# A two-layer graph attention kernel: row masks in pieces of 512 columns behind the second exponential, and the values of two steps gathered together

## The chip, the cores and the metric

The kernel runs on one core of a Trainium2 chip. The metric is the device time of one launch in microseconds (us); lower is better. TensorE is called PE here, VectorE DVE, ScalarE ACT, GpSimd POOL; SP is the engine that issues the DMAs.

## What is computed

Two layers of the same form stand one behind the other, with N = 4096 nodes, 128 features, 8 heads of 16 and an adjacency matrix of 4096 x 4096 that masks the scores:

```python
qkv = layer_norm(x, g1, be1) @ w_qkv
qkv = qkv.reshape(n, 3, HEADS, HEAD_DIM)
q, k, v = (qkv[:, 0], qkv[:, 1], qkv[:, 2])
scores = jnp.einsum('nhd,mhd->hnm', q, k) * SCALE
mask = (adj != 0)[None, :, :]
scores = jnp.where(mask, scores, -jnp.inf)
attn = jax.nn.softmax(scores, axis=-1)
out = jnp.einsum('hnm,mhd->nhd', attn, v).reshape(n, DIM)
x = x + out @ w_proj + b_proj
h2 = layer_norm(x, g2, be2)
ff = jax.nn.gelu(h2 @ w1 + b1) @ w2 + b2
return x + ff
```

All of it is in float32.

## The kernel before

Each layer has three phases with a barrier between them: `project` makes queries, keys and values, `attend` is the attention, `feed_forward` the rest. Nearly all the time lies in `attend`, and the change touches nothing else.

The 4096 queries are cut into 8 blocks of 512 (`NB`), the keys into 32 slices of 128 (`MT`). `attend` does two kinds of work side by side.

The **max jobs** find the largest masked score of each query and head. A job is one matmul of 128 queries by 512 keys for one head (`a_job`, L386) into one of three PSUM banks (`A_BANKS`), and one custom instruction of DVE, with a read of its accumulator, that subtracts the row mask `mask_n` and takes the maximum (`take_max`, L736). A block has 256 jobs. After them DVE splits the maxima (`split_neg`), and four more jobs, called turns, transpose them (L393) and add them to the queries (`add_neg`). The row masks are made by ACT from loaded rows of the adjacency matrix, 1024 columns at a time (`mask_rows`, L624), in two slots; a piece serves 16 jobs.

The **steps** do the attention itself: 512 a layer (`STEPS`), 64 to a block, each with four heads (the first 32 steps of a block, its first half, have heads 0 to 3, the others heads 4 to 7) and one slice of 128 keys. In `b_step` PE first runs two max jobs, then computes the scores of heads 0 and 1 (L414) when the first exponential of the step before is done, adds the mask to them by a matmul with the identity (L420), then the scores of heads 2 and 3 when the second exponential of the step before is done, and a second part of the mask; then two more max jobs; and at the end `gather_v` of the step two before (`LAG`), which multiplies the probabilities by the values (L407), four matmuls side by side in four column strips, each of which the trace shows as two instructions:

```python
                if t >= LAG:
                    gather_v(L, t - LAG)
```

ACT takes two exponentials of 1024 columns a step (`exp_pair`, L608), the first of heads 0 and 1, the second of heads 2 and 3. POOL then multiplies the values of heads 2 and 3 by a mask of zeros and ones (`mask_pair`, L860), in place of the full mask matmul for these heads. In the first layer's first halves POOL also makes the masks from the adjacency matrix (L844, L850) and multiplies in every second step only, and PE adds the full mask in the others. `p_buf` has four slots. At the start of each half, in the step whose number divides by 32 with remainder 2, ACT copies the finished output of the half before (`keep_o`, L616) between the two exponentials; the first gather of a half waits for that copy.

The jobs run ahead of the steps by a block and some (`FIRST_JOBS`): 276 of them before the first step. So the last block of steps of each layer has no jobs beside it; there a step has another form, with the mask by matmuls of full height (L460).

Each engine works through its own queue in the order of the code. What binds them are semaphores, and where a mask piece stands on ACT follows from numbers: `chunk_step(i)` is the step in which PE reaches the first job of piece i, and `attend` of ACT makes the piece two steps ahead:

```python
                    exp_pair(L, t, 0)
                    if t > LAG and t % MT == LAG:
                        keep_o(L, t // MT - 1)
                    while chunk[0] < NCH and chunk_step(chunk[0]) - 2 < t + 1:
                        mask_rows(L, chunk[0])
                        chunk[0] += 1
                    exp_pair(L, t, 1)
```

SP issues all loads and stores from one sorted list, in which a load of adjacency rows (`load_n`) is due nine steps ahead of its jobs.

Of the kernel before, what the change touches and what calls it, by code (L numbers as in the profile page):

```python
# [27 lines left out]
NB = N // TILE  # L28
NS = TILE // P
MT = N // P  # L30
CHUNK = 1024
NC = N // CHUNK


# [6 lines left out]
P_SLOTS = 4  # L41
Q_SLOTS = 3
M_SLOTS = 6
LAG = 2
LEAD = 16

# [28 lines left out]


def chunk_jobs(nb, q, c):
    return JOB_AT["score", nb, q, 2 * c, 0], JOB_AT["score", nb, q, 2 * c + 1, HEADS - 1]


C_QK, C_V, C_PROJ, C_W1, C_W2 = 0, 1024, 1152, 1280, 1792
# [5 lines left out]
def gnn_kernel(nc, x, adj, adj_t, weights, signs, ident, ident_f, out):  # L87
    ctx = ExitStack()
    with ctx:
        def sb(name, shape, dt):  # L90
            return ctx.enter_context(nc.sbuf_tensor(name, shape, dt))
# [17 lines left out]
        q_t = sb("q_t", [P, Q_SLOTS, PAIRS, TILE], F32R)  # L109
        v_sb = sb("v_sb", [P, MT * HEADS * VW + 16], F32)  # L110
        v_rows = v_sb[:, 0:MT * HEADS * VW].rearrange("p (t h d) -> p t h d", t=MT, d=VW)
        adj_in = sb("adj_in", [P, 2, CHUNK], I32)
        mask01 = sb("mask01", [P, M_SLOTS, TILE], I32)
        mask_n = sb("mask_n", [P, 2, CHUNK], BF16)
        spill = sb("spill", [P, A_BANKS, TILE], BF16)
        pmax = sb("pmax", [P, 2, NS * HEADS, 8], F32)
        neg = sb("neg", [P, NS * HEADS], F32)
# [46 lines left out]
        q_stored = [sem("q_stored_0"), sem("q_stored_1")]  # L164

        q_loaded = [sem(f"q_loaded_{i}") for i in range(Q_SLOTS)]
        adj_loaded = [sem("adj_loaded_0"), sem("adj_loaded_1")]
        adjt_loaded = [sem(f"adjt_loaded_{i}") for i in range(M_SLOTS)]
        n_made, mask01_made, t_made, p_masked = sem("n_made"), sem("mask01_made"), sem("t_made"), sem("p_masked")
        m01_stored, mt_stored = [sem(f"m01_stored_{i}") for i in range(M_SLOTS)], sem("mt_stored")  # L170
# [46 lines left out]
        def _(sp):  # L217
# [5 lines left out]
            def load_n(L, i):  # L223
                sub, c = i // NC, i % NC
                gi = L * NCH + i
                if gi >= 2:
                    sp.wait_ge(n_made, gi - 1)
                sp.dma_start(adj_in[:, gi % 2, :], adj[sub * P:(sub + 1) * P, c * CHUNK:(c + 1) * CHUNK]).then_inc(adj_loaded[gi % 2], 16)

            def load_t(L, t):  # L230
                nb, s, slot = t // (2 * MT), t % MT, t % M_SLOTS
# [40 lines left out]
            for L in range(LAYERS):  # L272
# [17 lines left out]
                sp.wait_ge(q_stored[1], (L + 1) * NB // 2 * 16)  # L290
                phase_barrier(sp, 3 * L + 1)

                order = [(chunk_step(i) - 9, "n", i) for i in range(NCH)]
                order += [(t - M_SLOTS + 2.2, "t", t) for t in range(STEPS)]
                if L == 0:
                    order += [(t - 1, "s", t) for t in range(STEPS) if made(L, t)]
# [44 lines left out]
        def _(pe):  # L341
# [81 lines left out]
            def b_step(L, t):  # L423


                nb, quad, s = t // (2 * MT), t // MT % 2, t % MT
                jobs = range(jobs_before(t), jobs_before(t + 1))
                for j in jobs[:2]:
                    a_job(L, j)
                if L == 0:  # L430
                    pe.wait_ge(t_made, nb * MT + s + 1)
                else:
                    pe.wait_ge(mt_loaded[s % 4], (nb * MT + s) // 4 * 16 + 16)
                if t > 0:
                    pe.wait_ge(b_exped, L * 2 * STEPS + 2 * t - 1)
                if s == 0:
                    pe.wait_ge(a_done, L * NJ + JOB_AT["turn", nb, 2 * quad + 1] + 1)
                score_b(L, t, 0), score_b(L, t, 1)
                if len(jobs) >= 4:
                    add_mask(s, 0, 0), add_mask(s, 1, 1).then_inc(half_added, 1)  # L440
                    added[0] += 1
                    if t > 0:
                        pe.wait_ge(b_exped, L * 2 * STEPS + 2 * t)
                    score_b(L, t, 2), score_b(L, t, 3)
                    pe.wait_ge(half_added, added[0])
                    if pooled(L, t):
                        add_mask(s, 1, 0), add_mask(s, 0, 1).then_inc(b_scored, 2)
                        for j in jobs[2:]:
                            a_job(L, j)
                    else:  # L450
                        add_mask(s, 1, 0), add_mask(s, 0, 1).then_inc(b_scored, 1)
                        add_mask(s, 2, 0), add_mask(s, 3, 1).then_inc(half_added, 1)
                        added[0] += 1
                        for j in jobs[2:]:
                            a_job(L, j)
                        pe.wait_ge(half_added, added[0])
                        add_mask(s, 3, 0), add_mask(s, 2, 1).then_inc(b_scored, 1)
                else:
                    for j in range(2):
                        mm = pe.matmul(ps_b[:, j, :], idb[:], mask_t[:, s, :], start=False, stop=True)  # L460
                    mm.then_inc(b_scored, 1)
                    for j in jobs[2:]:
                        a_job(L, j)
                    if t > 0:
                        pe.wait_ge(b_exped, L * 2 * STEPS + 2 * t)
                    score_b(L, t, 2)
                    mm = score_b(L, t, 3)
                    if not pooled(L, t):
                        for j in range(2, 4):
                            mm = pe.matmul(ps_b[:, j, :], idb[:], mask_t[:, s, :], start=False, stop=True)  # L470
                    mm.then_inc(b_scored, 1)
                if t >= LAG:
                    gather_v(L, t - LAG)

            def attend(L):
# [85 lines left out]
        def _(act):  # L561
# [55 lines left out]

            def mask_rows(L, i):
                gi = L * NCH + i
                act.wait_ge(adj_loaded[gi % 2], (gi // 2 + 1) * 16)  # L620
                if i >= 2:
                    j = i - 2
                    act.wait_ge(a_done, L * NJ + chunk_jobs(j // NC // NS, j // NC % NS, j % NC)[1] + 1)
                nc.scalar.activation(mask_n[:, gi % 2, :], adj_in[:, gi % 2, :].bitcast(U32), ACT.Exp,  # L624
                                     bias=far[:], scale=MASKED).then_inc(n_made, 1)

            def attend(L):
                chunk = [0]
                while chunk_step(chunk[0]) < 1:
                    mask_rows(L, chunk[0])  # L630
                    chunk[0] += 1
                for t in range(STEPS):
                    exp_pair(L, t, 0)
                    if t > LAG and t % MT == LAG:
                        keep_o(L, t // MT - 1)
                    while chunk[0] < NCH and chunk_step(chunk[0]) - 2 < t + 1:
                        mask_rows(L, chunk[0])
                        chunk[0] += 1
                    exp_pair(L, t, 1)
                keep_o(L, 2 * NB - 1)  # L640

            def keep_attn(gi):
# [33 lines left out]
        def _(dve):  # L676
# [52 lines left out]

            def take_max(L, j):  # L730
                kind, nb, q, mb, h = JOBS[j]
                if h == 0 and mb % 2 == 0:
                    dve.wait_ge(n_made, L * NCH + (nb * NS + q) * NC + mb // 2 + 1)
                ca = L * NCH + (nb * NS + q) * NC + mb // 2
                dve.wait_ge(a_scored, L * NJ + j + 1)
                dve.tensor_tensor_reduce(spill[:, j % A_BANKS, :], ps_a[:, j % A_BANKS, :],  # L736
                                         mask_n[:, ca % 2, (mb % 2) * TILE:(mb % 2 + 1) * TILE],
                                         1.0, LOWEST, ALU.subtract, ALU.max,
                                         pmax[:, nb % 2, q * HEADS + h, mb:mb + 1]).then_inc(a_done, 1)

# [190 lines left out]
```

## Time and profile before

| | us |
|---|---|
| median of 3 runs | 4095.02 |
| lowest, highest | 4086.28, 4095.74 |
| the profiled execution, its own time | 4093.91 |
| its span, from the first to the last instruction | 4092.1 |
| busy: PE, DVE, POOL, ACT | 3621.1, 2945.0, 2481.3, 2445.5 |
| mean granted clock of PE, as a share of 2.4 GHz | 0.927 |

The page gives busy time, the chain of work that ended last, and the costliest groups of instructions. The timeline lists the instructions in order of time: start, length, engine, line, and in brackets how long the engine had been idle and what released it. Neighbours of one kind are merged, with their count. Starts of matmuls can be trusted more than their ends, which are modelled; so the text reads the distance from start to start.

### The profile page before, as it was taken

To read this page: it belongs to the slowest core of one execution; us is meant where nothing else is said; L and a number is where in the kernel's file an instruction comes from. 1 tells how busy PE (TensorE), PEld (TensorE's weight loads), DVE (VectorE), ACT (ScalarE), POOL (GpSimd) and SP (SyncE) were. 2 spreads that over 40 slices of the span, in tenths; PEclk is the share of its full clock that TensorE was granted. 3 is DMA by queue.
4 is the path that set the end of the run, shared out by engine and by line. 5 is a ranking of instruction groups with operands and counts; after the bars stand their busy time and mean duration, and the time that the engine had idled before them with its cause. 6 is when DMAs were issued, how large, how long until landed. Compare 5 with 4: busy or idle time off the path is not lost.

```text
span 4092.1 us, 66045 instructions
## 1 busy us (share of the span) xinstructions
PE 3621.1 (88%) x22382; PEld 1452.0 (35%) x22416; DVE 2945.0 (72%) x8933; ACT 2445.5 (60%) x2596; POOL 2481.3 (61%) x1476
## 2 busy tenths in 40 slices
PE   6999898989998989898679999889989998999976
PEld 3443333333333333323434433333333333333234
DVE  6998888888888888701368988888888888886013
ACT  5126666666666666675241166766676767676842
POOL 1017777777777777786010077777777777777940
PEclk9559999999999999998885599999999999999988
DMA  3236574747474747372232254545454545453421
GB/s 136 78 104 224 157 227 150 234 142 239 139 241 140 244 132 250 106 226 79 60 102 91 92 154 142 159 152 157 141 159 148 160 140 161 147 159 116 139 68 57
DMA packets 332878, 608.98 MB, mean 149 GB/s; under 512 B 35169, under 2 KB 125409, under 8 KB 328161
## 3 DMA queue, kind: packets, MB, share of 16 engines
q1 hardware_dynamic: 332112, 604.65, 46.8%
q8 instruction: 183, 3.00, 0.3%
q14 instruction: 151, 1.23, 0.1%
q10 hardware_dynamic: 432, 0.10, 0.0%
HBM read 474.59 MB, written 132.12 MB: 148 GB/s over the span
## 4 chain that ended last, share of the span: by engine, by line
POOL 34%; PE 29%; issue 18%; DVE 10%; ACT 6%; DMA 1%; POOLq 1%; DVEq 0%; SPq 0%; ACTq 0%
POOL arena L860 34%; DVE spill L736 9%; PE PS L407 8%; PE PS L386 6%; PE PS L414 6%; PE PS L420 5%; ACT mask_n L624 3%; PE PS L359 3%; ACT arena L608 2%; PE PS L393 1%; POOLq L838 1%; DVE neg_hi L745 0%; DVE arena L699 0%; PE PS L460 0%; DMA adj_in<-in_adj 0%
## 5 line engine op out<-in xcount | busy, mean ns | idle before, releaser
L736 DVE CUSTOM_DVE_ANT_0 spill<-PS,mask_n 128x512 bf16<-128x512 f32 x4096 | 2614.5, 688 | 480.1 <-PE PS L386 421.9
L860 POOL TENSOR_TENSOR arena<-arena,mask 128x1024 int32<-128x1024 int32 x896 | 2129.9, 2377 | 948.4 <-ACT arena L608 943.6
L608 ACT ACTIVATE arena<-PS 128x1024 f32<-128x1024 f32 x2048 | 2013.4, 1022 | 1013.5 <-PE PS L420 936.1
L386 PE MATMUL PS<-k_t,q_t 48*128 48x512 f32 x4096 | 1355.4, 564 | 60.9 <-DVE pmax L736 44.3
L407 PE MATMUL PS<-arena,v_sb 128*32 128x512 f32 x8192 | 1101.6, 610 | 42.1 <-POOL arena L860 33.0
L414 PE MATMUL PS<-q_t,k_t 50*128 50x512 f32 x4096 | 944.9, 469 | 189.1 <-ACT arena L608 188.7
L386 PEld LDWEIGHTS PS<-k_t,q_t 48*128 48x128 f32 x4096 | 586.0, 202 | 1023.9 <-DVE pmax L736 959.3
L420 PE MATMUL PS<-arena,idb 64*128 64x512 bf16 x4000 | 783.4, 393 | 0.0
L414 PEld LDWEIGHTS PS<-q_t,k_t 50*128 50x128 f32 x4096 | 396.3, 189 | 504.4 <-ACT arena L608 361.2
L624 ACT ACTIVATE mask_n<-adj_in,far 128x1024 bf16<-128x1024 uint32 x256 | 291.9, 1141 | 284.2 <-DVE pmax L736 276.9
L420 PEld LDWEIGHTS PS<-arena,idb 64*128 64x128 bf16 x4000 | 193.0, 96 | 436.1 <-issue 312.0
L736 DVE DVE_READ_ACCUMULATOR2_ANT pmax<- 128x1 f32 x4096 | 339.5, 83 | 0.0
L778 DVE RECIPROCAL arena<-PS 128x32 f32<-128x32 f32 x16 | 5.7, 357 | 443.2 <-PE PS L491 443.2
L844 POOL TENSOR_SCALAR mask<-mask 128x512 int32<-128x512 uint32 x256 | 156.9, 613 | 202.1 <-DMA mask<-in_adj_t 192.6
L407 PEld LDWEIGHTS PS<-arena,v_sb 128*32 128x32 f32 x8192 | 162.6, 108 | 322.3 <-issue 269.3
L833 POOL TENSOR_SCALAR arena<-arena 128x4 f32<-128x4 f32 x32 | 7.3, 228 | 403.1 <-DVE arena L690 403.1
L850 POOL TENSOR_SCALAR arena<-mask 128x512 bf16<-128x512 int32 x256 | 158.1, 618 | 37.6 <-POOL mask L844 34.1
L359 PE MATMUL PS<-arena,wts 128*128 128x512 f32 x256 | 115.5, 605 | 0.0
L570 ACT ACTIVATE arena<-PS,wts 128x512 f32<-128x512 f32 x32 | 24.9, 777 | 145.1 <-PE PS L512 99.5
L652 ACT ACTIVATE arena<-PS,wts 128x512 f32<-128x512 f32 x64 | 43.8, 687 | 106.2 <-PE PS L520 103.7
L491 PE MATMUL PS<-idf,arena 128*128 128x128 f32 x128 | 31.3, 427 | 68.2 <-DMA arena<-attn_dram 68.2
L460 PE MATMUL PS<-arena,idb 128*128 128x512 bf16 x238 | 74.6, 384 | 5.4 <-issue 5.4
(54 smaller groups left out, 1022.7 us busy)
## 6 DMA issues: line engine op xcount, KB each, us to landing
mask<-m_dram SPq DMA_DIRECT2D x768, 256.0 KB, 2.7
adj_in<-in_adj SPq DMA_DIRECT2D x256, 512.0 KB, 3.9
mask<-in_adj_t SPq DMA_DIRECT2D x256, 256.0 KB, 3.8
m_dram<-mask SPq DMA_DIRECT2D x256, 256.0 KB, 3.5
mt_dram<-arena SPq DMA_DIRECT2D x256, 128.0 KB, 3.2
arena<-mt_dram SPq DMA_DIRECT2D x256, 128.0 KB, 2.7
q_dram<-arena SPq DMA_DIRECT2D x16, 1024.0 KB, 4.5
q_t<-q_dram SPq DMA_DIRECT2D x16, 1024.0 KB, 6.8
```

The source lines that it names most:

```text
L359: pe.matmul(PS[:, 2 + i % 4, :], wts[:, C_QK + i * P:C_QK + (i + 1) * P], xn_t[:, gx % 2, :], start=True, stop=True).then_inc(qk_ready, 1)
L386: pe.matmul(bank, q_t[r0:r0 + KROWS, (L * NB + nb) % Q_SLOTS, pair, q * P:(q + 1) * P], k_t[r0:r0 + KROWS, pair, mb * TILE:(mb + 1) * TILE ...
L407: mm = pe.matmul(ps_o[32 * j:32 * j + 32, :], v_sb[:, (s * HEADS + h) * VW:(s * HEADS + h) * VW + 32], p_buf[:, t % P_SLOTS, j, :], start= ...
L414: return pe.matmul(ps_b[:, j, :], k_t[r0:r0 + BROWS, pair, s * P:(s + 1) * P], q_t[r0:r0 + BROWS, (L * NB + nb) % Q_SLOTS, pair, :], start ...
L420: return pe.matmul(ps_b[:, j, :], idb[r0:r0 + 64, :], mask_t[r0:r0 + 64, s, :], start=False, stop=part != j % 2)
L460: mm = pe.matmul(ps_b[:, j, :], idb[:], mask_t[:, s, :], start=False, stop=True)
L608: nc.scalar.activation(p_buf[:, t % P_SLOTS, 2 * half:2 * half + 2, :], ps_b[:, 2 * half:2 * half + 2, :], ACT.Exp, scale=SCALE).then_inc( ...
L624: nc.scalar.activation(mask_n[:, gi % 2, :], adj_in[:, gi % 2, :].bitcast(U32), ACT.Exp, bias=far[:], scale=MASKED).then_inc(n_made, 1)
L736: dve.tensor_tensor_reduce(spill[:, j % A_BANKS, :], ps_a[:, j % A_BANKS, :], mask_n[:, ca % 2, (mb % 2) * TILE:(mb % 2 + 1) * TILE], 1.0, ...
L844: pool.tensor_scalar(m, m.bitcast(U32), 1.0, 0.0, ALU.min, ALU.max).then_inc(mask01_made, 1)
L850: pool.tensor_scalar(mask_t[:, s, :], m, -MASKED, MASKED, ALU.mult, ALU.add).then_inc(t_made, 1)
L860: pool.tensor_tensor(p, p, m, ALU.mult).then_inc(p_masked, 1)
```

## The change

It has two parts. Both are in `attend`.

**Row masks.** `CHUNK` falls from 1024 to 512, so that a piece serves 8 jobs and there are 256 pieces a layer in place of 128; the slots go from two to four (`N_SLOTS`), of half the size each. On ACT a piece now stands behind the second exponential of a step and three steps ahead of its jobs. SP loads it ten steps ahead.

**Values.** PE gathers in odd steps only, and then for two steps: those three and two before.

```diff
-CHUNK = 1024
+CHUNK = 512
+N_SLOTS = 4
...
-    return JOB_AT["score", nb, q, 2 * c, 0], JOB_AT["score", nb, q, 2 * c + 1, HEADS - 1]
+    return JOB_AT["score", nb, q, c, 0], JOB_AT["score", nb, q, c, HEADS - 1]
...
-        adj_in = sb("adj_in", [P, 2, CHUNK], I32)
+        adj_in = sb("adj_in", [P, N_SLOTS, CHUNK], I32)
-        mask_n = sb("mask_n", [P, 2, CHUNK], BF16)
+        mask_n = sb("mask_n", [P, N_SLOTS, CHUNK], BF16)
...
-                if gi >= 2:
-                    sp.wait_ge(n_made, gi - 1)
-                sp.dma_start(adj_in[:, gi % 2, :], adj[sub * P:(sub + 1) * P, c * CHUNK:(c + 1) * CHUNK]).then_inc(adj_loaded[gi % 2], 16)
+                if gi >= N_SLOTS:
+                    sp.wait_ge(n_made, gi - N_SLOTS + 1)
+                sp.dma_start(adj_in[:, gi % N_SLOTS, :],
+                             adj[sub * P:(sub + 1) * P, c * CHUNK:(c + 1) * CHUNK]).then_inc(adj_loaded[gi % N_SLOTS], 16)
...
-                order = [(chunk_step(i) - 9, "n", i) for i in range(NCH)]
+                order = [(chunk_step(i) - 10, "n", i) for i in range(NCH)]
...
-                if t >= LAG:
+                if t % 2 == 1 and t > LAG:
+                    gather_v(L, t - LAG - 1)
                     gather_v(L, t - LAG)
...
-                act.wait_ge(adj_loaded[gi % 2], (gi // 2 + 1) * 16)
-                if i >= 2:
-                    j = i - 2
+                slot = gi % N_SLOTS
+                act.wait_ge(adj_loaded[slot], (gi // N_SLOTS + 1) * 16)
+                if i >= N_SLOTS:
+                    j = i - N_SLOTS
...
-                while chunk_step(chunk[0]) < 1:
+                while chunk_step(chunk[0]) < 3:
...
-                    while chunk[0] < NCH and chunk_step(chunk[0]) - 2 < t + 1:
+                    exp_pair(L, t, 1)
+                    while chunk[0] < NCH and chunk_step(chunk[0]) - 3 < t + 1:
                         mask_rows(L, chunk[0])
                         chunk[0] += 1
-                    exp_pair(L, t, 1)
...
-                if h == 0 and mb % 2 == 0:
-                    dve.wait_ge(n_made, L * NCH + (nb * NS + q) * NC + mb // 2 + 1)
-                ca = L * NCH + (nb * NS + q) * NC + mb // 2
+                ca = L * NCH + (nb * NS + q) * NC + mb
+                if h == 0:
+                    dve.wait_ge(n_made, ca + 1)
```

The order of PE's queue in the second layer, before: one step, from its first max jobs (L386) over scores (L414) and masks (L420) to the gather (L407).

```order
L386 MATMUL PS<-k_t,q_t 128x512 x2
L414 MATMUL PS<-q_t,k_t 128x512 x2
L420 MATMUL PS<-arena,idb 128x512 x2
L414 MATMUL PS<-q_t,k_t 128x512 x2
L420 MATMUL PS<-arena,idb 128x512 x2
L386 MATMUL PS<-k_t,q_t 128x512 x2
L407 MATMUL PS<-arena,v_sb 32x512 x4
```

The same place in the changed kernel, where the lines are two further down: two steps, an even one without and an odd one with a gather of eight matmuls.

```order
L388 MATMUL PS<-k_t,q_t 128x512 x2
L416 MATMUL PS<-q_t,k_t 128x512 x2
L422 MATMUL PS<-arena,idb 128x512 x2
L416 MATMUL PS<-q_t,k_t 128x512 x2
L422 MATMUL PS<-arena,idb 128x512 x2
L388 MATMUL PS<-k_t,q_t 128x512 x4
L416 MATMUL PS<-q_t,k_t 128x512 x2
L422 MATMUL PS<-arena,idb 128x512 x2
L416 MATMUL PS<-q_t,k_t 128x512 x2
L422 MATMUL PS<-arena,idb 128x512 x2
L388 MATMUL PS<-k_t,q_t 128x512 x2
L409 MATMUL PS<-arena,v_sb 32x512 x8
```

The gather of the even step has gone into the odd one, and the last two jobs of the even step now stand directly ahead of the first two of the odd step.

The order of ACT's queue in the second layer about a copy of the output (L616), before: exponentials are L608, mask pieces L624.

```order
L624 ACTIVATE mask_n<-adj_in,far 128x1024
L608 ACTIVATE arena<-PS 128x1024 x2
L616 COPY o_sb<-PS 128x512
L608 ACTIVATE arena<-PS 128x1024 x6
L624 ACTIVATE mask_n<-adj_in,far 128x1024
```

The same place in the changed kernel (exponentials L611, copy L619, mask pieces L628):

```order
L628 ACTIVATE mask_n<-adj_in,far 128x512
L611 ACTIVATE arena<-PS 128x1024 x3
L619 COPY o_sb<-PS 128x512
L611 ACTIVATE arena<-PS 128x1024
L628 ACTIVATE mask_n<-adj_in,far 128x512
L611 ACTIVATE arena<-PS 128x1024 x4
```

A piece now follows four exponentials, or two steps, and the copy, which belongs to an even step, is followed by that step's second exponential and then by a piece: the pieces stand at the end of even steps.

## Rows read from the trace of the kernel before

**Rows 1.** The page, part 1: busy us, share of the span, instructions

```profile
PE 3621.1 (88%) x22382; PEld 1452.0 (35%) x22416; DVE 2945.0 (72%) x8933; ACT 2445.5 (60%) x2596; POOL 2481.3 (61%) x1476
```

**Rows 2.** The page, part 4: shares of the chain that ended last

```profile
POOL 34%; PE 29%; issue 18%; DVE 10%; ACT 6%; DMA 1%; POOLq 1%; DVEq 0%; SPq 0%; ACTq 0%
```

**Rows 3.** Timeline, second layer: start, us, engine, line, op, out<-in, count, idle before

```profile
3011.01 1.94 ACT L608 ACTIVATE arena<-PS 128x1024 f32<-128x1024 f32 x2 [0.82 <-PE PS L420]
...
3011.14 1.07 PE L407 MATMUL PS<-arena,v_sb 128*32 128x512 f32 x8
...
3012.14 0.50 PE L386 MATMUL PS<-k_t,q_t 48*128 48x512 f32 x2
...
3012.47 0.40 PE L414 MATMUL PS<-q_t,k_t 50*128 50x512 f32 x2
...
3013.00 0.50 PE L414 MATMUL PS<-q_t,k_t 50*128 50x512 f32 x2
...
3013.35 0.39 PE L420 MATMUL PS<-arena,idb 64*128 64x512 bf16 x2
...
3013.78 1.03 ACT L608 ACTIVATE arena<-PS 128x1024 f32<-128x1024 f32 x1 [0.83 <-PE PS L420]
...
3014.70 1.14 ACT L624 ACTIVATE mask_n<-adj_in,far 128x1024 bf16<-128x1024 uint32 x1
...
3017.58 1.94 ACT L608 ACTIVATE arena<-PS 128x1024 f32<-128x1024 f32 x2 [0.82 <-PE PS L420]
```

**Rows 4.** Groups by line: out<-in shapes xcount, busy, mean ns, idle before

```profile
L624 ACT ACTIVATE mask_n<-adj_in,far 128x1024 bf16<-128x1024 uint32 x256 | 291.9, 1141 | 284.2 <-DVE pmax L736 276.9
...
L583 ACT ACTIVATE arena<-PS,sgn 128x512 fp32r<-128x512 f32 x64 | 44.0, 687 | 12.4 <-PE PS L359 12.4
```

**Rows 5.** Chain in order of time, start of the first layer's attention

```profile
103.68 6.44 DMA adj_in<-in_adj
```

**Rows 6.** Timeline: second wave of a gather, and the job behind it

```profile
2999.49 0.61 PE L407 MATMUL PS<-arena,v_sb 128*32 128x512 f32 x4
...
3000.04 0.50 PE L386 MATMUL PS<-k_t,q_t 48*128 48x512 f32 x2
```

**Rows 7.** Timeline, first layer: scores, and the next first exponential

```profile
805.79 0.40 PE L414 MATMUL PS<-q_t,k_t 50*128 50x512 f32 x2
...
806.94 1.94 ACT L608 ACTIVATE arena<-PS 128x1024 f32<-128x1024 f32 x2 [0.88 <-PE PS L420]
```

**Rows 8.** Stretches: busy us (count) of PE, PEld, DVE, ACT, POOL; PEclk, DMA

```profile
2997.05:3057.00 59.95, 55.17 (x400) 20.60 (x400) 51.34 (x161) 43.42 (x46) 47.15 (x21) 1.00 0.50 157
```

**Rows 9.** Timeline, first layer, first half: gathers four steps apart

```profile
999.82 1.07 PE L407 MATMUL PS<-arena,v_sb 128*32 128x512 f32 x8
...
1012.55 0.64 PE L407 MATMUL PS<-arena,v_sb 128*32 128x512 f32 x4
```

**Rows 10.** Timeline, last block without max jobs: one step

```profile
1869.62 0.50 PE L414 MATMUL PS<-q_t,k_t 50*128 50x512 f32 x2
...
1870.05 0.61 PE L460 MATMUL PS<-arena,idb 128*128 128x512 bf16 x2
...
1870.59 0.50 PE L414 MATMUL PS<-q_t,k_t 50*128 50x512 f32 x2
...
1870.69 1.94 ACT L608 ACTIVATE arena<-PS 128x1024 f32<-128x1024 f32 x2 [0.46 <-PE PS L460]
...
1871.02 1.06 PE L407 MATMUL PS<-arena,v_sb 128*32 128x512 f32 x8
```

**Rows 11.** Timeline, change of half: copy, second exponential, waiting gather

```profile
814.42 0.58 ACT L616 COPY o_sb<-PS 128x512 f32<-128x512 f32 x1
...
814.89 1.04 ACT L608 ACTIVATE arena<-PS 128x1024 f32<-128x1024 f32 x1
...
815.15 1.06 PE L407 MATMUL PS<-arena,v_sb 128*32 128x512 f32 x8 [1.46 <-POOL arena L860]
```

**Rows 12.** Stretches, columns as in rows 8: after the stall of a block change

```profile
3147.00:3152.00 5.00, 5.00 (x32) 3.04 (x32) 2.35 (x5) 1.08 (x2) 0.18 (x1) 0.66 0.27 79
```

More of the change, by code:

```diff
@@ L166, in gnn_kernel @@
         q_loaded = [sem(f"q_loaded_{i}") for i in range(Q_SLOTS)]
-        adj_loaded = [sem("adj_loaded_0"), sem("adj_loaded_1")]
+        adj_loaded = [sem(f"adj_loaded_{i}") for i in range(N_SLOTS)]
         adjt_loaded = [sem(f"adjt_loaded_{i}") for i in range(M_SLOTS)]
@@ L619, in mask_rows @@
                 gi = L * NCH + i
-                act.wait_ge(adj_loaded[gi % 2], (gi // 2 + 1) * 16)
-                if i >= 2:
-                    j = i - 2
+                slot = gi % N_SLOTS
+                act.wait_ge(adj_loaded[slot], (gi // N_SLOTS + 1) * 16)
+                if i >= N_SLOTS:
+                    j = i - N_SLOTS
                     act.wait_ge(a_done, L * NJ + chunk_jobs(j // NC // NS, j // NC % NS, j % NC)[1] + 1)
-                nc.scalar.activation(mask_n[:, gi % 2, :], adj_in[:, gi % 2, :].bitcast(U32), ACT.Exp,
+                nc.scalar.activation(mask_n[:, slot, :], adj_in[:, slot, :].bitcast(U32), ACT.Exp,
                                      bias=far[:], scale=MASKED).then_inc(n_made, 1)
@@ L731, in take_max @@
                 kind, nb, q, mb, h = JOBS[j]
-                if h == 0 and mb % 2 == 0:
-                    dve.wait_ge(n_made, L * NCH + (nb * NS + q) * NC + mb // 2 + 1)
-                ca = L * NCH + (nb * NS + q) * NC + mb // 2
+                ca = L * NCH + (nb * NS + q) * NC + mb
+                if h == 0:
+                    dve.wait_ge(n_made, ca + 1)
                 dve.wait_ge(a_scored, L * NJ + j + 1)
                 dve.tensor_tensor_reduce(spill[:, j % A_BANKS, :], ps_a[:, j % A_BANKS, :],
-                                         mask_n[:, ca % 2, (mb % 2) * TILE:(mb % 2 + 1) * TILE],
+                                         mask_n[:, ca % N_SLOTS, :],
                                          1.0, LOWEST, ALU.subtract, ALU.max,
```

## Prediction

> **What bounds the kernel now.** I read the busy shares first, then the chain, then the timeline of single steps. No engine is full: PE 88%, DVE 72%, POOL 61%, ACT 60% [rows 1]. The chain puts 34% on POOL's multiplication and 29% on PE [rows 2], which looks like a POOL bound, but the timeline says otherwise. Rows 3 show an ordinary step of the second layer, and every step of that kind reads the same. ACT starts the two exponentials of a step at 3011.01; one row shows both, 1.94 us together. At 3013.00 PE starts the scores of heads 2 and 3 of the next step, which need the second exponential; at 3013.35 it adds the mask; at 3013.78 ACT starts again, having idled 0.8 us. So the loop is ACT, PE, ACT, and takes 2.77 us. Beside it PE runs its own row of work in those same 2.77 us: gather at 3011.14, two max jobs at 3012.14, scores at 3012.47, some 0.25 us for the mask, and then a wait of only about 0.2 us for ACT. Two limits thus stand almost level: **ACT's loop at 2.77 us, and PE's queue at about 2.7 us**. Every fourth step is longer: 1024 columns of row masks (1.14 us) stand on ACT between the two exponentials, and the step takes 3.80 us (3013.78 to 3017.58) [rows 3]. Four steps take 3 x 2.77 + 3.80 = 12.1 us, or 6.05 a pair.
>
> **Part one, the masks move and are halved.** The second exponential no longer stands behind a mask, which takes away 1.03 us from every fourth step. What is late next there is the ordinary loop of 2.77. A piece of 512 columns now stands behind the second exponential in every second step. The order puts it into even steps nearly throughout (the copy of o_sb, in a step that divides to 2, comes two instructions ahead of one). There ACT idles 0.8 us. How long does a piece take? From below, half of 1.14, or 0.57; from above 1.14; the nearest row is an activation of 512 columns with a bias operand, 0.69 us [rows 4], which I take. It overlaps its neighbour by some 0.1 us, as the second exponential starts 0.92 after the first, so it ends within the idle time; at 1.14 it would run 0.1 us or so over. The skill gives the same: the Trainium skill (ScalarE: Activation LUTs, What ACT_TABLE_LOAD costs) states about 280 ns + 0.833 ns an element with a bias operand, which is 1133 ns for 1024 columns, where this trace has 1141, and an estimate of 707 ns for 512. The 256 additional DMA issues lie on SP's queue, whose issues are not on the chain but for the first; 2 KB rows take the place of 4 KB ones. Masks wait for work of DVE four pieces back, about eight steps, and are loaded seven steps before use: no new wait. The very first load of a layer is on the chain for 6.44 us [rows 5] with four loads of 512 KB issued in a row; with half the bytes I estimate 2 us less, so **-4 us** for both layers (between 0 and -6).
>
> **Part two, two gathers in a row.** This removes one gather (about 1.0 us of PE) from every even step and puts it into the odd one. In an even step the first limit, ACT's loop, stays: 2.77 us, and PE idles a good microsecond. In an odd step PE's queue decides. What does the second gather add? A gather is two waves of four matmuls; the second wave starts at 2999.49 and the next job at 3000.04 [rows 6], so 0.55 of the 1.00 us from 3011.14 to 3012.14 [rows 3] is second wave and way out, 0.45 the first. Two more waves at 0.45 add 0.91, and the way out is paid once: 1.90 us for both. At the worst it adds a whole 1.00. Then, from the start of the first exponential of an odd step: 0.13 to the gather, 1.90, then 0.33 for two jobs up to the scores [rows 3], then from those scores to the next exponential where PE does not wait, 805.79 to 806.94, or 1.15 [rows 7]. That makes **3.51 us**. With the even step, 3.51 + 2.77 = **6.28 us a pair against 6.05**: the loss of overlap costs more than the mask stall gave.
>
> What the page on tiling says speaks for the change: the Trainium skill (TensorEngine Tiling (Array Packing), Key Properties) states that a change of tiling mode drains TensorE, and a gather is in another mode than all around it, so paired gathers halve such changes. The rows show a drain of about 0.1 us at the way out, which the 1.90 has already credited; if the drain were nothing, the pair would be at 6.37.
>
> DVE: 80 jobs of two instructions took 51.3 us in a stretch of 60 [rows 8], 0.64 each, so 8 want 5.1 of the 6.28 us. While PE gathers twice, DVE has three banks at most and idles about a microsecond. In the even step four jobs then stand in a row on PE, the last of which waits until DVE has done two of them; it comes about when the first exponential ends, for which PE would wait anyway. I take 0, and 0.1 us a pair at the worst. POOL gets more time: 4.8 us of work a pair, and values of an even step are needed one step later.
>
> **The sum.** Seven of eight column blocks of each layer carry max jobs.
> - Second layer and second halves of the first: 224 + 112 pairs x 0.23 = **+77**.
> - First halves of the first layer, where POOL also makes masks: from gather to gather four steps take 12.73 us [rows 9], 6.36 a pair; the new odd and even steps have the same limits as above, 6.28: 112 x -0.08 = **-9**.
> - Blocks without jobs (the last, 64 steps a layer): a step is 2.40 now. PE's row of work there, with s for scores and m for masks: 1.00 for the gather as in rows 3, 0.43 s, 0.54 m, 0.43 to the gather [rows 10]. With two gathers: 0.43 + 1.90 + 0.43 + 0.54 = 3.30 from the second scores to the next. In the even step the first scores wait for an exponential that starts 0.1 after and takes 1.02, then 0.43 and 0.54: 2.15. Together 5.45 against 4.80: 48 pairs x 0.65 = **+31**; the 16 pairs of the first layer's first half, slower already, I count at nothing (up to +10).
> - Change of half: the output is copied on ACT and the next gather waits 1.46 us for it [rows 11], on PE's path. Now the copy runs in an even step and the gather comes a step later, so only the 0.47 stays by which the second exponential starts later. 14 changes x -1.0, and two in the last blocks: **-16**.
> - Change of block: PE waits for DVE's maxima, and POOL works 0.18 us of 5 [rows 12]. Copy and jobs shift somewhat within that stall: 0, with 14 x 1.46, or 20 us, either way.
> - First loads **-4**.
> Sum 77 - 9 + 31 - 16 - 4 = **+79**. The profiled execution took 4093.9 us, about 1 us less than the median of the runs, so I forecast **4174 us**, 1.9% slower.
>
> **Rivals.**
> (1) The second gather is covered, so that both steps stay at ACT's 2.77, and only the mask stall goes. For it: the chain names POOL and ACT far more than gathers. It would give 168 groups of four steps x 1.02 and 56 x 1.65 less, -264 us with the -20 above: about 3810. Against it: PE waits 0.2 us in a step, not 0.9. Between this and the forecast lies every case in which the second gather adds less; the point from which the sign turns is 79 / 464 pairs = 0.17 below 0.91, that is 0.74 us for two waves that take 0.91 now. Chance 0.09 for faster, 0.06 for within 0.3%, about what a measurement can tell from no change.
> (2) PE's clock falls. After the stall at a change of block the granted clock is 0.66 in 5 us [rows 12], between the levels 2.4 and 1.2 GHz, and matmuls take up to twice as long. PE would now idle a good microsecond in 6.3, against about one in 12 now. If one pair in ten ran at the lower level, its 3.4 us of PE work in the odd step doubles: 46 x 3.4 = +156, so 4330. Against it: the present stalls of about 1 us behind the masks left the clock at 1.00 in that stretch [rows 8]. The Trainium skill (TensorE: Matmul & The Clock Gate, A second HAM failure mode: psum-queue depth-cycling) tells of a kernel whose clock oscillated through frequent short idles; no row here shows it. Chance 0.08.
> (3) The mask piece does not fit into the idle time of the even step (its first wait is for a load or for DVE, or it takes 1.14): 0.1 us in 448 pairs, +45, 4220. Chance 0.07.
> (4) The forecast as worked out, chance 0.70.
>
> **Chances and range.** Faster 0.09, within 0.3% 0.06, slower 0.85. The second gather at 1.00 gives +42, DVE's banks +45, blocks -20 to +20, tail -15 to +10, first loads a little: 4135 to 4235 about the forecast. To leave out two in ten I take 4125 to 4240.
>
> **What would show it.** First exponentials of a pair 3.5 and 2.8 us apart, gathers as 16 matmuls within 1.9 us with no wait ahead, then scores, and ACT idling some 1.6 us in odd steps for PE's mask matmul; no mask piece between two exponentials, each some 0.7 us; PE's busy share down, POOL idling 0.7 us a step; steps of the last block 3.3 and 2.15; no gather waiting for a copy. It is wrong if the odd step takes under 3.3 us, if the even one takes over 2.9 (DVE or masks), or if the granted clock falls below 0.9 in mid block.

## The result and the profile after

The changed kernel takes 4167.35 us (median of 4 runs, 4159.95 to 4176.57) against 4094.52 us before: the ratio is 1.018, with a 95% interval of 1.016 to 1.021. It is slower by 73 us. The forecast was 4174 us, in a range of 4125 to 4240.

The page of the changed kernel, part 1 (busy us, share of the span) and part 4 (shares of the chain):

```profile
PE 3772.3 (91%) x22416; PEld 1603.9 (39%) x22416; DVE 2906.9 (70%) x8933; ACT 2495.9 (60%) x2852; POOL 2480.3 (60%) x1476
...
POOL 33%; PE 30%; issue 19%; DVE 15%; DMA 1%; ACT 1%; POOLq 1%; DVEq 0%; SPq 0%; ACTq 0%
```

They answer to [rows 1, 2], and neither tells what happened. The shares of the chain differ by five points at most, and PE's busy share has even risen, from 88 to 91%. The timeline of the second layer tells it; here are an even and an odd step of the changed kernel, and the start of the next even one. Columns: start, length, engine, line, form, count, idle before.

```profile
3041.75 1.94 ACT L611 ACTIVATE arena<-PS 128x1024 f32<-128x1024 f32 x2 [1.53 <-PE PS L422]
...
3043.57 0.72 ACT L628 ACTIVATE mask_n<-adj_in,far 128x512 bf16<-128x512 uint32 x1
3043.74 0.19 PEld L416 LDWEIGHTS PS<-q_t,k_t 50*128 50x128 f32 x2 [0.30 <-ACT arena L611]
...
3044.51 1.94 ACT L611 ACTIVATE arena<-PS 128x1024 f32<-128x1024 f32 x2 [0.22 <-PE PS L422]
3044.64 1.92 PE L409 MATMUL PS<-arena,v_sb 128*32 128x512 f32 x16
...
3046.49 0.51 PE L388 MATMUL PS<-k_t,q_t 48*128 48x512 f32 x2
...
3046.84 0.40 PE L416 MATMUL PS<-q_t,k_t 50*128 50x512 f32 x2
...
3047.59 1.91 PE L388 MATMUL PS<-k_t,q_t 48*128 48x512 f32 x4
...
3047.98 1.94 ACT L611 ACTIVATE arena<-PS 128x1024 f32<-128x1024 f32 x2 [1.53 <-PE PS L422]
```

The even step runs from 3041.75 to 3044.51, 2.76 us. Its mask piece stands behind both exponentials, takes 0.72 us, and ACT still idles 0.22 us. PE waits 0.30 us for the second exponential there (3043.74; PEld is PE's weight load), so ACT's loop sets this step. The odd step runs to 3047.98, 3.47 us: PE gathers from 3044.64 to 3046.49, then makes two jobs, scores and masks, and ACT idles 1.53 us. The pair is 6.23 us against 6.05 before [rows 3]. The row at 3047.59 also shows why PE's busy share rose. Four max jobs in a row are listed with 1.91 us, where two take 0.50: the weight loads of the third and fourth wait for DVE, 0.43 us each, and the merged row counts that as busy.

The place that answers to [rows 11], the change of half:

```profile
2889.31 1.02 ACT L611 ACTIVATE arena<-PS 128x1024 f32<-128x1024 f32 x1 [1.52 <-PE PS L422]
2890.23 0.58 ACT L619 COPY o_sb<-PS 128x512 f32<-128x512 f32 x1
2890.70 1.04 ACT L611 ACTIVATE arena<-PS 128x1024 f32<-128x1024 f32 x1
...
2892.57 1.94 ACT L611 ACTIVATE arena<-PS 128x1024 f32<-128x1024 f32 x2 [0.23 <-PE PS L422]
2892.70 1.92 PE L409 MATMUL PS<-arena,v_sb 128*32 128x512 f32 x16
```

This even step takes 3.26 us, 0.50 more than an ordinary one, and the gather at 2892.70 waits for nothing. Not every change of half went so well. In seven of the fourteen beside max jobs, and at the start of two blocks, TensorE's granted clock fell to the level of 1.2 GHz for a few us, and the odd step behind the copy took 4.6 to 5.2 us, in place of 3.47 at a change of half. One such place, the gather and the stretch about it (span, busy us of PE, PEld, DVE, ACT, POOL, then the granted clock), and for comparison a stretch in mid block:

```profile
1022.82 3.48 PE L409 MATMUL PS<-arena,v_sb 128*32 128x512 f32 x16
...
1022.70:1026.20 3.50, 3.50 (x18) 0.59 (x16) 1.31 (x4) 1.94 (x2) 3.11 (x2) 0.55 0.60 173
3050.00:3110.00 60.00, 57.38 (x390) 22.84 (x390) 47.85 (x153) 43.35 (x49) 45.94 (x20) 1.00 0.49 141
```

The kernel before had such falls too, at four changes of half and the start of one block, all in the second layer. At a change of block PE waits for DVE in both kernels, 2.81 us before and 2.80 now at the places shown. Two gathers now stand behind this wait, and they run at the lower level. The gather behind the wait before, then in the changed kernel, with the clock of its stretch:

```profile
3146.21 1.06 PE L407 MATMUL PS<-arena,v_sb 128*32 128x512 f32 x8
...
3179.60 3.64 PE L409 MATMUL PS<-arena,v_sb 128*32 128x512 f32 x16
...
3178.00:3182.00 4.00, 3.12 (x13) 0.88 (x17) 2.53 (x8) 0.43 (x1) 2.25 (x1) 0.50 0.59 161
```

The last block, which answers to [rows 10]:

```profile
3990.91 1.94 ACT L611 ACTIVATE arena<-PS 128x1024 f32<-128x1024 f32 x2 [0.30 <-PE PS L462]
3994.17 1.94 ACT L611 ACTIVATE arena<-PS 128x1024 f32<-128x1024 f32 x2 [1.32 <-PE PS L462]
3996.40 1.94 ACT L611 ACTIVATE arena<-PS 128x1024 f32<-128x1024 f32 x2 [0.30 <-PE PS L462]
```

3.26 and 2.23 us, 5.49 a pair against 4.80.

### The profile page after: what moved, and what is told of

It is laid out like the page before. It is cut to its first block, busy times and chain, and to the rows that moved or that the text cites. A ratio compares the mean times of both kernels' runs of the same rounds, so it can differ in the third digit from the quotient of the medians.

```text
span 4165.8 us, 67099 instructions
## 1 busy us (share of the span) xinstructions
PE 3772.3 (91%) x22416; PEld 1603.9 (39%) x22416; DVE 2906.9 (70%) x8933; ACT 2495.9 (60%) x2852; POOL 2480.3 (60%) x1476
## 4 chain that ended last, share of the span: by engine, by line
POOL 33%; PE 30%; issue 19%; DVE 15%; DMA 1%; ACT 1%; POOLq 1%; DVEq 0%; SPq 0%; ACTq 0%
POOL arena L864 33%; DVE spill L740 13%; PE PS L409 10%; PE PS L388 7%; PE PS L416 5%; PE PS L422 4%; PE PS L361 3%; ACT arena L611 1%; DVE pmax L740 1%; POOLq L842 1%; PE PS L395 0%; DVE arena L703 0%; DVE neg_hi L749 0%; PE PS L462 0%; DMA adj_in<-in_adj 0%
## 5 line engine op out<-in xcount | busy, mean ns | idle before, releaser
L740 DVE CUSTOM_DVE_ANT_0 spill<-PS,mask_n 128x512 bf16<-128x512 f32 x4096 | 2580.8, 688 | 533.1 <-PE PS L388 494.5
L611 ACT ACTIVATE arena<-PS 128x1024 f32<-128x1024 f32 x2048 | 1991.2, 1022 | 1047.5 <-PE PS L422 935.5
L388 PE MATMUL PS<-k_t,q_t 48*128 48x512 f32 x4096 | 1583.9, 568 | 161.7 <-DVE pmax L740 70.5
L416 PE MATMUL PS<-q_t,k_t 50*128 50x512 f32 x4096 | 1020.1, 483 | 53.8 <-ACT arena L611 51.9
L388 PEld LDWEIGHTS PS<-k_t,q_t 48*128 48x128 f32 x4096 | 659.5, 202 | 1006.2 <-DVE pmax L740 942.0
L409 PE MATMUL PS<-arena,v_sb 128*32 128x512 f32 x8192 | 1019.1, 616 | 2.6 <-POOL arena L864 2.5
L422 PE MATMUL PS<-arena,idb 64*128 64x512 bf16 x4000 | 836.8, 391 | 0.0
L628 ACT ACTIVATE mask_n<-adj_in,far 128x512 bf16<-128x512 uint32 x512 | 369.9, 723 | 271.6 <-DVE pmax L740 265.1
L409 PEld LDWEIGHTS PS<-arena,v_sb 128*32 128x32 f32 x8192 | 217.4, 111 | 489.6 <-issue 474.5
L422 PEld LDWEIGHTS PS<-arena,idb 64*128 64x128 bf16 x4000 | 231.5, 95 | 408.8 <-issue 180.1
L762 DVE TENSOR_TENSOR q_t<-PS,q_t 128x512 fp32r<-128x512 f32 x64 | 42.1, 688 | 59.9 <-PE PS L395 59.5
```

The costliest lines, as they stand in the source:

```text
L388: pe.matmul(bank, q_t[r0:r0 + KROWS, (L * NB + nb) % Q_SLOTS, pair, q * P:(q + 1) * P], k_t[r0:r0 + KROWS, pair, mb * TILE:(mb + 1) * TILE ...
L409: mm = pe.matmul(ps_o[32 * j:32 * j + 32, :], v_sb[:, (s * HEADS + h) * VW:(s * HEADS + h) * VW + 32], p_buf[:, t % P_SLOTS, j, :], start= ...
L416: return pe.matmul(ps_b[:, j, :], k_t[r0:r0 + BROWS, pair, s * P:(s + 1) * P], q_t[r0:r0 + BROWS, (L * NB + nb) % Q_SLOTS, pair, :], start ...
L422: return pe.matmul(ps_b[:, j, :], idb[r0:r0 + 64, :], mask_t[r0:r0 + 64, s, :], start=False, stop=part != j % 2)
L611: nc.scalar.activation(p_buf[:, t % P_SLOTS, 2 * half:2 * half + 2, :], ps_b[:, 2 * half:2 * half + 2, :], ACT.Exp, scale=SCALE).then_inc( ...
L628: nc.scalar.activation(mask_n[:, slot, :], adj_in[:, slot, :].bitcast(U32), ACT.Exp, bias=far[:], scale=MASKED).then_inc(n_made, 1)
```

## The experiments

The theory to test: the two parts work against each other. The masks' new place is a large gain; the paired gathers lose more than that, because a gather costs nothing beside the exponentials as long as PE has one a step, and PE's queue sets the step when it has two. The rivals: that the masks are what made it slower, or brought nothing; and that ACT's 1.5 us of idle time in the odd step is slack.

### The masks alone

```diff
-                if t % 2 == 1 and t > LAG:
-                    gather_v(L, t - LAG - 1)
+                if t >= LAG:
                     gather_v(L, t - LAG)
```

(against the changed kernel)

> The masks of the change, the gathers of the kernel before (one in every step). My theory: the mask stall of 1.03 us in every fourth step goes and nothing takes its place, since ACT's loop stays at 2.77 us and PE's queue at 2.7; four steps 11.1 us instead of 12.1, 168 x 1.0 + 56 x 1.0 = -225 us, about 3865 us. Rival A (max jobs and DVE come next at once): 11.3 us for four steps, about 3910. Rival B (the stall was cover for other work, so the masks bring nothing by themselves): about 4090.

Measured: **3874.88 us**, ratio to before 0.946 (0.944 to 0.948). This part alone is worth 222 us, 5.4%. ACT's rows of this kernel:

```profile
2700.84 1.94 ACT L610 ACTIVATE arena<-PS 128x1024 f32<-128x1024 f32 x2 [0.22 <-PE PS L422]
2703.60 1.94 ACT L610 ACTIVATE arena<-PS 128x1024 f32<-128x1024 f32 x2 [0.82 <-PE PS L422]
2705.43 0.72 ACT L627 ACTIVATE mask_n<-adj_in,far 128x512 bf16<-128x512 uint32 x1
2706.36 1.94 ACT L610 ACTIVATE arena<-PS 128x1024 f32<-128x1024 f32 x2 [0.21 <-PE PS L422]
2709.14 1.94 ACT L610 ACTIVATE arena<-PS 128x1024 f32<-128x1024 f32 x2 [0.84 <-PE PS L422]
2710.97 0.72 ACT L627 ACTIVATE mask_n<-adj_in,far 128x512 bf16<-128x512 uint32 x1
2711.91 1.03 ACT L610 ACTIVATE arena<-PS 128x1024 f32<-128x1024 f32 x1 [0.22 <-PE PS L422]
```

Four steps take 2711.91 - 2700.84 = 11.07 us, 2.77 each, with a piece in every second idle time. Nothing takes the place of the stall.

### The gathers alone

```diff
-                if t >= LAG:
+                if t % 2 == 1 and t > LAG:
+                    gather_v(L, t - LAG - 1)
                     gather_v(L, t - LAG)
```

(against the kernel before)

> The gathers of the change, the masks of the kernel before (1024 columns between the exponentials). My theory: an odd step is set by PE at 3.47 us, or by ACT at 3.80 where a mask piece stands in it, an even one stays at 2.77; the pieces fall into odd steps nearly throughout, so four steps take 3.80 + 2.77 + 3.47 + 2.77 = 12.8 us against 12.1: +119 us, +4 in the first layer's first halves, +33 in the last blocks, -16 at the changes of half: about 4235 us. Rival (a second gather is covered, and the slowdown of the change comes from the masks): about 4080 us.

Measured: **4259.49 us**, ratio 1.040 (1.038 to 1.041), 162 us slower; the rival is out. ACT's rows:

```profile
2893.72 1.14 ACT L625 ACTIVATE mask_n<-adj_in,far 128x1024 bf16<-128x1024 uint32 x1
2894.76 1.01 ACT L609 ACTIVATE arena<-PS 128x1024 f32<-128x1024 f32 x1
2896.59 1.94 ACT L609 ACTIVATE arena<-PS 128x1024 f32<-128x1024 f32 x2 [0.82 <-PE PS L420]
2899.36 1.94 ACT L609 ACTIVATE arena<-PS 128x1024 f32<-128x1024 f32 x2 [0.83 <-PE PS L420]
2902.83 1.94 ACT L609 ACTIVATE arena<-PS 128x1024 f32<-128x1024 f32 x2 [1.53 <-PE PS L420]
2905.59 1.03 ACT L609 ACTIVATE arena<-PS 128x1024 f32<-128x1024 f32 x1 [0.83 <-PE PS L420]
2906.51 1.14 ACT L625 ACTIVATE mask_n<-adj_in,far 128x1024 bf16<-128x1024 uint32 x1
```

From the mask piece to the next one are four steps: 2906.51 - 2893.72 = 12.79 us, as expected. The piece falls into an odd step, where PE would have taken 3.47 us anyway, so it adds only some 0.33 us instead of 1.03.

That explains why the parts do not add up. Pairing the gathers costs 162 us where the mask stall is still there, and 4167 - 3875 = 292 us where it is gone: the old stall had covered part of it. In four steps pairing adds 12.79 - 12.10 = 0.69 us with the stall there, and 12.46 - 11.07 = 1.39 without it. Masks -222 and gathers +162 would give -60; the two together gave +73.

The total came out 24 us above my 4235. The four-step sum was right. Some 14 of the 24 us lie at the changes of block, for which I had nothing: the four steps about PE's wait took 23 us more than before at the fourteen of them, where the four-step sum gives 10. The changes of half, where I had carried over a gain of 16, came out as expected in their sum; most of the rest lies in ordinary steps. In this kernel TensorE's granted clock stood at the 1.2 GHz level for 123 us between the first and last exponentials of the two attentions, in place of 79 before.

### A third gather

```diff
                 if t % 2 == 1 and t > LAG:
                     gather_v(L, t - LAG - 1)
-                    gather_v(L, t - LAG)
+                    gather_v(L, t - LAG, twice=True)
...
-                for j in range(4):
+                for j in 2 * list(range(4)) if twice and s < MT - 1 else range(4):
```

(against the changed kernel)

> The changed kernel with the gather of the odd step's own values done twice (the result of it is another: these values count twice), in 15 of 16 odd steps. My theory: PE's queue sets the odd step, so two more waves add their whole 0.87 us each time: 480 x 0.87 = +415 us, about 4580 us. Rival (ACT's idle time of 1.5 us in the odd step is slack that PE can use): 4167 us plus next to nothing.

Measured: **4579.65 us**, 412 us above the changed kernel, for 480 gathers: 0.86 us each (median of 2 runs). The timeline:

```profile
2949.99 1.94 ACT L611 ACTIVATE arena<-PS 128x1024 f32<-128x1024 f32 x2 [0.22 <-PE PS L422]
2950.11 2.78 PE L409 MATMUL PS<-arena,v_sb 128*32 128x512 f32 x24
2954.30 1.94 ACT L611 ACTIVATE arena<-PS 128x1024 f32<-128x1024 f32 x2 [2.37 <-PE PS L422]
```

ACT's idle time grows from 1.53 to 2.37 us, by about as much as PE's row of gathers (1.92 to 2.78). It is no slack that PE could use: it is ACT waiting for PE. In the odd step each wave of PE's gather is on the path in full.

### The old pieces in the new place, and the new pieces in the old place

The first has the kernel before with its 1024 columns, but behind the second exponential:

```diff
-                    while chunk[0] < NCH and chunk_step(chunk[0]) - 2 < t + 1:
+                    exp_pair(L, t, 1)
+                    while chunk[0] < NCH and chunk_step(chunk[0]) - 2 < t + 1:
                         mask_rows(L, chunk[0])
                         chunk[0] += 1
-                    exp_pair(L, t, 1)
```

> The kernel before, but its 1024-column pieces stand behind the second exponential; everything else as before. My theory: the piece takes 1.14 us of which 0.1 overlaps, and finds 0.83 us of idle time, so every fourth step is some 0.2 us late instead of 1.03: four steps 11.3 us, -0.82 x 224 = -184 us, about 3910 us. Against the masks alone in 512 columns this says what the narrower pieces are worth: about 45 us. Rival (position alone does it, width nothing): the same time as the masks alone. Rival (width alone does it): about 4090 us.

Measured: **3887.40 us**, ratio 0.949 (0.948 to 0.950), only 12 us behind the narrow pieces. I had over-estimated the lateness of a wide piece:

```profile
2740.06 1.94 ACT L608 ACTIVATE arena<-PS 128x1024 f32<-128x1024 f32 x2 [0.83 <-PE PS L420]
2741.89 1.15 ACT L624 ACTIVATE mask_n<-adj_in,far 128x1024 bf16<-128x1024 uint32 x1
2742.93 1.94 ACT L608 ACTIVATE arena<-PS 128x1024 f32<-128x1024 f32 x2
```

The step is 2.87 us instead of 2.77. The piece overlaps the exponentials at both its ends, starting 0.1 us before the one ahead is over and followed by the next 1.04 after its start. I had taken off only one overlap.

The second has the masks-alone kernel with each piece between the exponentials:

```diff
+                    while chunk[0] < NCH and chunk_step(chunk[0]) - 3 < t + 1:
+                        mask_rows(L, chunk[0])
+                        chunk[0] += 1
                     exp_pair(L, t, 1)
-                    while chunk[0] < NCH and chunk_step(chunk[0]) - 3 < t + 1:
-                        mask_rows(L, chunk[0])
-                        chunk[0] += 1
```

> The 512-column pieces, four slots and earlier loads of the change, but each piece between the two exponentials as before, and one gather a step. It separates width from position. My theory (position does it): every second step is late by the piece's 0.72 less 0.1 of overlap, 0.62, so four steps take 11.08 + 1.24 = 12.3 us against 12.1: 168 x 0.2 = +37, about as much in the first layer's first halves, so 4130 to 4140 us. Rival (width or the slots do it): 3875 us as the masks alone, or somewhere between.

Measured: **4069.34 us**, ratio 0.994 (0.992 to 0.996). The ordinary pair is as I said, 6.14 us, slower than 6.05:

```profile
2901.70 1.94 ACT L610 ACTIVATE arena<-PS 128x1024 f32<-128x1024 f32 x2 [0.83 <-PE PS L422]
2904.46 1.03 ACT L610 ACTIVATE arena<-PS 128x1024 f32<-128x1024 f32 x1 [0.83 <-PE PS L422]
2905.39 0.71 ACT L627 ACTIVATE mask_n<-adj_in,far 128x512 bf16<-128x512 uint32 x1
...
2907.84 1.03 ACT L610 ACTIVATE arena<-PS 128x1024 f32<-128x1024 f32 x1 [0.83 <-PE PS L422]
```

But the total is 25 us faster than before, where I had expected it 35 to 45 slower. What I left out: in the first layer's first halves the pair is also 6.14, against 6.36 [rows 9], 21 us less in all. And at four changes of half of the second layer the step with the copy had taken 6.10 to 6.11 us before, with a granted clock of 0.53 at the first of them (2451.0 to 2456.2 us); it takes 4.12 here, as at all others beside max jobs. Still the reading holds: from here to the masks alone, which differ in the place of the piece only, are 194 us; width, slots and loads together are worth 12 to 25.

### The copy first

The paired gathers brought one thing, that no gather waits for the copy. Here is another way to it, on top of the masks alone:

```diff
-                    exp_pair(L, t, 0)
                     if t > LAG and t % MT == LAG:
                         keep_o(L, t // MT - 1)
+                    exp_pair(L, t, 0)
```

> The masks of the change, one gather a step, and the copy of the output ahead of the first exponential of its step instead of behind it. My theory: the gather before it has ended by then and the copy of 0.58 us fits into ACT's idle 0.83 us, so the first gather of a half no longer waits 1.46 us: 16 changes of half x 1.5 = -24 us against the masks alone, and up to as much at the changes of block: 3830 to 3850 us. It takes from the paired gathers the one thing they brought. Rival (the wait at a change of half has another cause): 3875 us.

Measured: **3838.65 us**, ratio 0.937 (0.936 to 0.939), 36 us below the masks alone. It is the fastest kernel of this study, 6.3% faster than before and 7.9% faster than the changed kernel. Its change of half:

```profile
2681.91 1.94 ACT L610 ACTIVATE arena<-PS 128x1024 f32<-128x1024 f32 x2 [0.22 <-PE PS L422]
2682.18 1.06 PE L409 MATMUL PS<-arena,v_sb 128*32 128x512 f32 x8
2683.74 0.59 ACT L618 COPY o_sb<-PS 128x512 f32<-128x512 f32 x1
2684.68 1.94 ACT L610 ACTIVATE arena<-PS 128x1024 f32<-128x1024 f32 x2 [0.35 <-PE PS L422]
2684.88 1.06 PE L409 MATMUL PS<-arena,v_sb 128*32 128x512 f32 x8
```

The step from 2681.91 to 2684.68 takes 2.77 us, as any other: the copy has gone into ACT's idle time. In the profiled executions the four steps at each change of half give 25 us in all, and those at the starts of blocks 10: there the step with the copy takes 3.33 us in the second layer, where it took 4.12, so the copy is not free in these places.

### Loosening ACT's loop

```diff
                     if pooled(L, t):
-                        add_mask(s, 1, 0), add_mask(s, 0, 1).then_inc(b_scored, 2)
+                        pe.wait_ge(half_added, added[0])
+                        add_mask(s, 1, 0), add_mask(s, 0, 1).then_inc(b_scored, 1)
+                        if t > 0:
+                            pe.wait_ge(b_exped, L * 2 * STEPS + 2 * t)
+                        score_b(L, t, 2)
+                        score_b(L, t, 3).then_inc(b_scored, 1)
                         for j in jobs[2:]:
                             a_job(L, j)
```

(against the kernel with the copy first; the wait for the second exponential and the scores of heads 2 and 3 stood ahead of this branch)

> As the kernel with the copy first, but in the steps that POOL masks PE adds the whole mask of heads 0 and 1 before it waits for the second exponential, and signals the two halves apart. It loosens ACT's loop, which is one of the two limits of a step. My theory: ACT is no longer a limit, and a step falls from 2.77 to PE's 2.7 us at best, some -0.05 x 670 steps = -35 us, about 3800 us; a wait of PE for its own first mask part (0.2 us or so) can eat it and more, up to 3900 us. Rival (PE's queue is not the second limit): steps of 2.4 to 2.5 us as POOL sets them, 3700 us or less.

Measured: **3883.77 us**, ratio 0.948 (0.947 to 0.950), 45 us slower than the kernel it starts from. Its ordinary steps of the second layer and of the first layer's second halves take 2.82 to 2.83 us, as these rows show; the first layer's first halves, where only every second step has the new order, stay at 5.87 a pair.

```profile
2701.14 1.94 ACT L615 ACTIVATE arena<-PS 128x1024 f32<-128x1024 f32 x2 [0.89 <-PE PS L422]
...
2703.54 0.10 PEld L422 LDWEIGHTS PS<-arena,idb 64*128 64x128 bf16 x2 [0.36 <-PE PS L422]
...
2703.97 1.94 ACT L615 ACTIVATE arena<-PS 128x1024 f32<-128x1024 f32 x2 [0.28 <-PE PS L422]
2704.01 0.40 PE L388 MATMUL PS<-k_t,q_t 48*128 48x512 f32 x2
...
2704.34 1.07 PE L409 MATMUL PS<-arena,v_sb 128*32 128x512 f32 x8
```

The step did not fall, but this does not settle the rival, since the edit puts a wait into PE's queue: PE waits for its own first mask part, 0.36 us at 2703.54. From 2725 to 2775 us, in 18 steps, this wait comes to 6.5 us, and PE waits for ACT not at all; in the same stretch of the masks alone it is 0.3 us, with 2.0 for ACT. The max jobs' banks hold up nothing here: the two jobs at 2704.01 take 0.33 us to the gather, as two jobs do in [rows 3]. So PE's queue sets the step here. Without its own wait it would stand at some 2.5 us (2.83 - 0.36, an estimate), not at the 2.7 of my theory, and whether steps of 2.4 to 2.5 us can be had is open.

## Why the prediction was right, point by point

- **Two limits almost level.** Right in what the forecast needs: the odd step follows PE when PE is given more (third gather). But 2.7 us for PE's queue was too high. The 2.77 us of [rows 3] less the wait of about 0.2 us for ACT are 2.57, and the last experiment gives about 2.5. The 3.51 us of the odd step do not use this number.
- **The mask stall goes, and an ordinary step is late next.** Right: 2.76 us with a piece in it, and by itself 222 us. The piece takes 723 ns in the changed kernel, where I took 687 from [rows 4]. The estimate from the Trainium skill (ScalarE: Activation LUTs, What ACT_TABLE_LOAD costs) was 707 ns; the trace has 16 ns more, and 0.22 us of idle time is left.
- **The odd step, 3.51 us.** Measured 3.47. The term that was off is the second gather: both take 1.85 us, from 3044.64 to 3046.49, not 1.90. What a further gather adds is then 0.85 to 0.86 us, as the third one shows too, and a gather alone costs 1.00 [rows 3]: about 0.14 us are paid once for a group, not 0.1. The Trainium skill (TensorEngine Tiling (Array Packing), Key Properties) says that a change of tiling mode drains TensorE, and that is in line with it, though no run here separates such a drain from other causes of the 0.14 us. Pairing saves this 0.14 us a pair, and loses the overlap of a whole gather.
- **The even step, 2.77 us.** Right, 2.76. DVE's banks cost nothing, though the fourth job waited: as I had it, PE waits for the exponential anyway, 0.30 us at 3043.74.
- **The sum.** Between the first exponentials of the first and the last step, the first layer's attention went from 1619.9 to 1639.2 us, by 19, and the second's from 1589.2 to 1642.7, by 54. My terms gave 26 - 9 + 10 - 8 = 19 for the first, and 51 + 21 - 8 = 64 for the second. The starts of the first exponentials split both (us; measured, and in brackets what my terms give for the same steps):

| steps | first layer | second layer |
|---|---|---|
| ordinary steps beside max jobs, 182 pairs | -4 (+12) | +27 (+42) |
| four steps about the wait at each change of block | +11 (+3) | +14 (+3) |
| four steps at each change of half | +3 (-4) | -9 (-4) |
| first four steps of each block | -2 (-1) | +3 (+5) |
| the rest of the last block | +11 (+9) | +19 (+18) |

So the mechanism and its price a pair were right, but that the total came within 7 us is in part luck. The ordinary steps fell 30 us short of my terms: a pair is 6.23, and 6.20 in the first layer's second halves, not 6.28, and the second halves had stood at 6.11 a pair on the mean before, not at 6.05. The changes of block, which I had put at 0, took 19 us more than my terms and made up for most of it, with the two gathers at the lower clock behind PE's wait. Single terms: the first halves of the first layer 6.23 against my 6.28 and 6.36 before; the last blocks 5.49 against 5.45; the first half of the first layer's last block, which I had counted at nothing, 5.49 against 5.33 before; the change of half 0.50 against 0.47. One count of the prediction is wrong: it divides 79 us by 464 pairs, where its own terms count 448 and 48, or 496; the turning point is then 0.16 us below 0.91, not 0.17.
- **First loads.** In the first layer DVE's first maximum came 3.3 us behind the first job's matmul before (108.22 to 111.49), and comes 2.0 us behind it now (107.29 to 109.27); in the second layer 4.6 us before (2164.08 to 2168.69) and 3.4 us now (2182.52 to 2185.94). A gain of 1.3 and 1.2 us, less than the 2 us a layer that I took.
- **Clock.** The rival did not come as I had put it: in mid block the granted clock is 1.00 (3050 to 3110 us), the 2.4 GHz level, although PE waits about a microsecond in every pair, in several pieces. But part of it came at the edges. Between the first and last exponentials of the two attentions the clock stood at the 1.2 GHz level for 113 us, against 79 before, at changes of block and of half, and the mean fell from 0.927 to 0.923. A paired gather took 1.92 and 3.64 us at the two levels, a factor of 1.9, so these 34 us more cost some 16 us at most, an estimate from these durations. Why the clock falls at some changes of half and not at others is open.
- **What was wrong** in the list of signs: I had expected PE's busy share to fall. It rose by 3 points, since the profile counts matmuls that are held up as busy. The counts and starts said what the share did not.

## What to carry to other kernels

Where two engines pass work to and fro, a step is the longer of the loop between them and of each one's own queue; work that has cover in every step loses it when it is bunched into every second one, since the short step cannot go below the loop and the long one pays in full. Measure the parts of a change apart: here one part alone gave 5.4% and the other took 7.5% from it, and the sum of their single effects had the wrong sign, since the stall that one part removed had been cover for the other. Put small work into the waits of its own engine: the same mask pieces cost 194 us between two exponentials and almost nothing behind them, and the copy was free one place earlier at the changes of half. Look at the edges too, and at the clock there: at the changes of block the paired gathers stood behind a wait of PE and ran at the lower level.

## What the hardware showed that I had not expected

- A 1024-column piece behind the exponentials delays the next step by 0.10 us only, although it takes 1.15 us where 0.83 us were idle: the piece overlaps the exponentials at both ends, by about 0.1 us each.
- A gather next to another costs 0.86 us, alone 1.00 us. The difference, 0.14 us, is more than what I could read off the first one's way out.
- TensorE's granted clock fell at changes of block and of half, and stood at 1.00 in the mid-block stretch shown. The same paired gather took 1.92 us at a granted clock of 1.00 and 3.64 us at 0.50 behind a wait of 2.8 us. The kernel with the copy first had no fall at any change of half, and stood at the lower level for 55 us of its attentions, against 113 in the changed kernel.
